# LoRA kernel, its tail: x and the product summed in PSUM for a tile and a half, and the last duo's split moved ahead

## The reference

```python
def _L0_cond_ref(x, A, B, adapter_ids):
    B_sel = B[adapter_ids]
    A_sel = A[adapter_ids]
    Bx = jnp.einsum('bni,bri->bnr', x, B_sel)
    out = jnp.einsum('bnr,bor->bno', Bx, A_sel)
    return out * SCALING          # SCALING = 1.0
x = x + _L0_cond_ref(x, L0_cond_A, L0_cond_B, itok_B_3_7)
```

## Time and profile before

| what | value |
|---|---|
| median of 3 runs | 93.06 us (93.05 to 93.09) |
| the profiled execution, whole time | 93.04 us |
| its span in the profile | 91.2 us |
| PE busy | 80.1 us (88%) |
| DVE busy | 59.7 us (65%) |
| ACT busy | 59.0 us (65%) |
| POOL busy | 60.3 us (66%) |
| DMA moved | 34.82 MB, mean 382 GB/s |

### The profile page before, as it was taken

One profiled execution on the slowest core, in us unless ns is written; L12 is line 12 of the kernel. 1 busy time (PEld: TensorE's weight loads), 2 busy tenths in 40 slices (PEclk: granted clock), 3 DMA queues, 4 the chain that ended last, 5 costly groups with the idle time before them and its releaser, 6 DMA issues.

```text
span 91.2 us, 3627 instructions
## 1 busy us (share of the span) xinstructions
PE 80.1 (88%) x1469; PEld 63.0 (69%) x1469; DVE 59.7 (65%) x106; ACT 59.0 (65%) x153; POOL 60.3 (66%) x136
## 2 busy tenths in 40 slices
PE   3999999999999999899999999999999999464400
PEld 3999988778687778587778687878787786322100
DVE  0039930359686768775959586776869696999900
ACT  1367698969696859396869596969695958131000
POOL 6000859999879697877878879797979793900000
PEclk9999999999999999999999999999999999999555
DMA  1899999999999999999999999999999999988890
GB/s 25 311 386 410 408 410 412 401 413 410 395 413 408 404 412 403 406 412 403 410 412 404 415 419 408 412 415 410 422 408 413 430 397 421 392 345 356 341 386 20
DMA packets 10193, 34.82 MB, mean 382 GB/s; under 512 B 834, under 2 KB 1858, under 8 KB 10178
## 3 DMA queue, kind: packets, MB, share of 16 engines
q1 hardware_dynamic: 10032, 34.08, 93.7%
q10 hardware_dynamic: 146, 0.52, 1.5%
HBM read 17.83 MB, written 16.78 MB: 380 GB/s over the span
## 4 chain that ended last, share of the span: by engine, by line
PE 85%; DVE 6%; issue 1%; ACT 1%; POOL 1%; POOLq 0%
PE t_bank L217 36%; PE y_banks L248 20%; PE bx_bank L228 20%; PE t_bank L187 5%; DVE x_all L361 4%; PE y_banks L206 4%; DVE bx_parts L352 2%; PE bx_bank L192 1%; ACT bx_parts L283 1%; POOL ident L140 0%; POOL ident L138 0%; POOLq L140 0%; POOLq L377 0%
## 5 line engine op out<-in xcount | busy, mean ns | idle before, releaser
L361 DVE TENSOR_TENSOR x_all<-y_banks,x_all 128x1024 f32<-128x1024 f32 x32 | 39.4, 1232 | 15.7 <-PE y_banks L248 15.1
L301 ACT COPY x_t<-t_bank 128x512 f32<-128x512 f32 x64 | 34.5, 592 | 13.9 <-PE t_bank L217 13.3
L166 POOL CAST a_duo<-a_table 128x512 fp32r x64 | 36.7, 615 | 3.1 <-PE y_banks L248 2.1
L217 PE MATMUL t_bank<-ident,x_all 128*128 128x128 f32 x256 | 34.9, 279 | 0.0
L156 POOL COPY b_duo<-b_table 128x256 f32 x64 | 22.8, 401 | 15.8 <-PE bx_bank L228 8.7
L217 PEld LDWEIGHTS t_bank<-ident,x_all 128*128 128x128 f32 x256 | 27.5, 141 | 7.0 <-issue 5.4
L248 PE MATMUL y_banks<-a_duo,bx_parts 64*128 64x512 f32 x128 | 20.6, 429 | 3.6 <-ACT bx_parts L283 3.2
L228 PE MATMUL bx_bank<-x_t,b_duo 128*32 128x64 f32 x1024 | 21.3, 222 | 0.0
L228 PEld LDWEIGHTS bx_bank<-x_t,b_duo 128*32 128x32 f32 x1024 | 16.1, 109 | 5.6 <-issue 5.2
L352 DVE TENSOR_TENSOR bx_parts<-bx_bank,bx_parts 32x64 fp32r<-32x64 f32 x64 | 14.1, 220 | 4.8 <-ACT bx_parts L316 3.7
L248 PEld LDWEIGHTS y_banks<-a_duo,bx_parts 64*128 64x128 f32 x128 | 10.9, 188 | 7.3 <-issue 3.8
(11 more groups left out here) (10 smaller groups left out, 4.9 us busy)
## 6 DMA issues: line engine op xcount, KB each, us to landing
out_y<-x_all SPq DMA_DIRECT2D x32, 512.0 KB, 13.2
x_all<-in_x SPq DMA_DIRECT2D x15, 1024.0 KB, 19.0
x_all<-in_x SPq DMA_DIRECT2D x2, 512.0 KB, 6.1
x_all<-in_B ACTq DMA_DIRECT2D x1, 512.0 KB, 4.3
x_all<-in_A SPq DMA_DIRECT2D x2, 256.0 KB, 4.8
id_row<-in_ids ACTq DMA_DIRECT2D x1, 0.2 KB
```

Of the source, the lines that this page charges most:

```text
L166: last = nc.gpsimd.tensor_copy(a_duo[duo % 2][:, k, :], a_table[:, bass.ds(adapters[k] * BANK, BANK)])
L217: last = nc.tensor.transpose(t_bank[unit % 2][:, c * P:(c + 1) * P], x_all[:, 2 * duo + tile, at:at + P], ident[:, :])
L301: nc.scalar.copy(x_t[duo % 2][:, half * HALF:(half + 1) * HALF, tile, :], t_bank[unit % 2][:, :].rearrange("p (c n) -> p c n", c=HALF)).th ...
L361: nc.vector.tensor_tensor(here, product, here, ALU.add).then_inc(y_drained, 1)
```

## The change

Only the tail is touched, duos 14 and 15. Line numbers of the changed kernel are higher by 9 on PE's loops, by 47 on ACT and by 56 on VectorE.

- Tile 29 (the second of duo 14) doesn't go through `y_banks` and VectorE any more. PE puts x itself into the two transpose banks, one matmul of the identity with 512 columns of x for each half (`x_into`), and adds the products of A onto it in the same banks. ACT copies the two sums to `x_all`, and the store waits for these copies (`sum_copied`).
- Tile 31 (the last) is cut in two. Its first half goes to `y_banks0` and VectorE as before, on 512 columns. Its second half is summed in `bx_bank0` as above and copied out by ACT.
- Tile 30 goes to `y_banks1` in place of `y_banks0`.
- ACT splits the last duo's B x (`split_high`) ahead of `double_parts` of duo 14, and VectorE does `split_rest` of duo 15 ahead of its add on tile 28.

The diff:

```diff
@@ -94,6 +94,8 @@
         parts_done = sem("parts_done")
         y_filled = sem("y_filled")
         y_drained = sem("y_drained")
+        sum_filled = sem("sum_filled")
+        sum_copied = sem("sum_copied")
 
         block = ctx.enter_context(nc.Block())
 
@@ -129,7 +131,14 @@
                     sp.wait_ge(a_filled, ADAPTERS)
                 sp.dma_start(x_all[:, first:end, :], rows[:, first:end, :]).then_inc(x_loaded[n], 16)
             for tile in range(TILES):
-                sp.wait_ge(y_drained, tile + 1)
+                if tile < TILES - 3:
+                    sp.wait_ge(y_drained, tile + 1)
+                elif tile == TILES - 3:
+                    sp.wait_ge(sum_copied, HALVES)
+                else:
+                    sp.wait_ge(y_drained, tile)
+                if tile == TILES - 1:
+                    sp.wait_ge(sum_copied, HALVES + 1)
                 sp.dma_start(out_rows[:, tile, :], x_all[:, tile, :]).then_inc(stored, 16)
             sp.wait_ge(stored, 16 * TILES)
 
@@ -269,9 +278,47 @@
                     transpose_unit(duo + 1, 2)
                     transpose_unit(duo + 1, 3)
                 down(duo, HALF, CHUNKS)
-                if duo:
+                if 0 < duo < DUOS - 1:
                     up(duo - 1)
-            up(DUOS - 1)
+            def product(bank, duo, k, h, start, stop):
+                ranks = slice(h * K_UP, (h + 1) * K_UP)
+                return nc.tensor.matmul(bank, bx_parts[duo % 2][ranks, k, :], a_duo[duo % 2][ranks, k, :],
+                                        start=start, stop=stop)
+
+            def x_into(bank, tile, h):
+                nc.tensor.matmul(bank, ident[:, :], x_all[:, tile, :].rearrange("n (o h) -> n h o", h=HALVES)[:, h],
+                                 start=True, stop=False)
+
+            before, end = DUOS - 2, DUOS - 1
+            for h in range(HALVES):
+                x_into(t_bank[h][:, :], TILES - 3, h)
+            pe.wait_ge(a_gathered, before + 1)
+            pe.wait_ge(parts_done, before + 1)
+            pe.wait_ge(y_drained, 2 * before - 1)
+            for s in range(PER_TILE):
+                for h in range(HALVES):
+                    last = product(y_banks[0][:, h * BANK:(h + 1) * BANK], before, s, h, s == 0, s == PER_TILE - 1)
+            last.then_inc(y_filled, 1)
+            for s in range(PER_TILE):
+                for h in range(HALVES):
+                    last = product(t_bank[h][:, :], before, PER_TILE + s, h, False, s == PER_TILE - 1)
+            last.then_inc(sum_filled, 1)
+
+            pe.wait_ge(a_gathered, end + 1)
+            pe.wait_ge(parts_done, end + 1)
+            pe.wait_ge(y_drained, 2 * before)
+            for s in range(PER_TILE):
+                for h in range(HALVES):
+                    last = product(y_banks[1][:, h * BANK:(h + 1) * BANK], end, s, h, s == 0, s == PER_TILE - 1)
+            last.then_inc(y_filled, 1)
+            pe.wait_ge(y_drained, 2 * before + 1)
+            for s in range(PER_TILE):
+                last = product(y_banks[0][:, 0:BANK], end, PER_TILE + s, 0, s == 0, s == PER_TILE - 1)
+            last.then_inc(y_filled, 1)
+            x_into(bx_bank[before % 2][:, :], TILES - 1, 1)
+            for s in range(PER_TILE):
+                last = product(bx_bank[before % 2][:, :], end, PER_TILE + s, 1, False, s == PER_TILE - 1)
+            last.then_inc(sum_filled, 1)
 
         @block.scalar
         def _(act):
@@ -325,13 +372,22 @@
                 if duo + 1 < DUOS:
                     copy_x(duo + 1, 0)
                     copy_x(duo + 1, 1)
+                if duo == DUOS - 1:
+                    split_high(duo)
                 if duo:
                     double_parts(duo - 1)
                 if duo + 1 < DUOS:
                     copy_x(duo + 1, 2)
                     copy_x(duo + 1, 3)
-                split_high(duo)
+                    split_high(duo)
             double_parts(DUOS - 1)
+            act.wait_ge(sum_filled, 1)
+            for h in range(HALVES):
+                nc.scalar.copy(x_all[:, TILES - 3, :].rearrange("n (o h) -> n h o", h=HALVES)[:, h],
+                               t_bank[h][:, :]).then_inc(sum_copied, 1)
+            act.wait_ge(sum_filled, 2)
+            nc.scalar.copy(x_all[:, TILES - 1, :].rearrange("n (o h) -> n h o", h=HALVES)[:, 1],
+                           bx_bank[(DUOS - 2) % 2][:, :]).then_inc(sum_copied, 1)
 
         @block.vector
         def _(dve):
@@ -361,12 +417,19 @@
                 nc.vector.tensor_tensor(here, product, here, ALU.add).then_inc(y_drained, 1)
 
             split_rest(0)
-            for duo in range(1, DUOS):
+            for duo in range(1, DUOS - 1):
                 add_x(duo - 1, 0)
                 split_rest(duo)
                 add_x(duo - 1, 1)
-            add_x(DUOS - 1, 0)
-            add_x(DUOS - 1, 1)
+            split_rest(DUOS - 1)
+            add_x(DUOS - 2, 0)
+            dve.wait_ge(y_filled, TILES - 2)
+            here = x_all[:, TILES - 2, :].rearrange("n (o h) -> n h o", h=HALVES)
+            product = y_banks[1][:, :].rearrange("n (h o) -> n h o", h=HALVES)
+            nc.vector.tensor_tensor(here, product, here, ALU.add).then_inc(y_drained, 1)
+            dve.wait_ge(y_filled, TILES - 1)
+            first_half = x_all[:, TILES - 1, :].rearrange("n (o h) -> n h o", h=HALVES)[:, 0]
+            nc.vector.tensor_tensor(first_half, y_banks[0][:, 0:BANK], first_half, ALU.add).then_inc(y_drained, 1)
 
 
 # ---- launch: one core; inputs and outputs as the reference has them ----
```

## The result

The changed kernel takes 93.28 us (median of 22 runs, 93.01 to 93.43) against 93.08 us for the kernel before in the same set (22 runs, 92.85 to 93.26). The ratio is 1.0018, 95% interval 1.0011 to 1.0026: by it 0.17 us slower. Two more sets, on other occasions, gave 1.0005 (0.9987 to 1.0022) and 1.0007 (0.9991 to 1.0022). So the last store's issue moved, and the time did not move down with it; whether it moved up by 0.1 to 0.2 us or not at all is at the edge of what can be measured; where the difference of the first set lies, the part on the cost of 0.17 us tells. The forecast was 93.05 and no change.

What follows compares the result with a forecast made beforehand. One DMA engine, behind by its own total, was taken to bound the kernel; tile 28's loss (0.93 us) cancels tile 29's gain for the others, so the sum is 0: 93.05 us, no change, range 92.6 to 93.3.

Steps and rivals of the forecast that it cites:

- What bounds the kernel: End of the span: one DMA engine of sixteen, behind by its own total, works alone over a microsecond, share 0.06.
- The slack that was read from the shares: Last stores: the last engine had tiles 29, 30 and 31 at hand each 1.6 us before it needed them.
- The sum of 0 for the change: Whole kernel: tile 28's loss cancels tile 29's gain and the last engine never waits; no change, chance 0.75.
- span 91.2, whole time 93.04: Last step of the sum: span and whole time with the change, against a median of 93.06, so 93.05 forecast.
- It never waits, and ends at 90.33: Last DMA engine in the changed tail: gets tiles 28 to 31 before needing them, so its end stays at 90.33.
- the landing of the last packet: End of the kernel: with small shifts between executions, the reason given for the forecast's own range, 92.9 to 93.2.
- The products with x: PE in the tail: identity times x on 512 columns, 0.85 us each; two take 1.7 us (1.0 to 2.3).
- The last store: Tile 31's store: issued at 85.4 us (85.0 to 85.9), 1.2 us earlier; SP's wait behind it 5.1 us.
- Tile 28 later by 0.93, the dry time only moved: Tile 28's add ends at 82.74, not 81.81; fifteen engines' dry time moves from 84.0-84.95 to 82.8-83.7.
- The end follows the last store: Rival, end of the kernel: the lone engine's lateness comes from the tail, so an earlier store gives 91.9; chance 0.13.
- x products that hold up tile 28: Rival, PE ahead of tile 28: slow x products (2.3 us each at the lower clock) delay its store, 94.3; chance 0.06.
- The instruction packets shift: Rival, DMA engines: last engine gains or loses 1.06 us of packet work, 94.1 or 91.9; chance 0.03 slower, 0.03 faster.

Runs made afterwards that it cites:

- the run with three spare adds: Kernel before with three spare VectorE adds of 128x1024, results unused, ahead of the last store's release (3.7 us planned delay): 95.33 us, ratio 1.0232.
- one add: Kernel before with one spare VectorE add of 128x1024, result unused, ahead of the last store's release: 93.11 us, ratio 1.0010.
- the three parts: Parts of the change, each alone in the kernel before: order of splits, ratio 0.9995; tile 29 by transpose banks and ScalarE, 0.9997; tile 31 cut in two, 1.0117.
- the part with the last tile alone: Kernel before with only tile 31 changed: second half summed with x in a down bank and copied by ScalarE: 94.35 us, ratio 1.0117.
- a version with fewer of them, at a lower precision: Kernel before with transposed x and gathered B kept in bf16, 7 instruction packets in place of 11: 91.40 us against 93.10, ratio 0.9820.
- the spare products: Kernel before with the change's three added fp32 products of 512 columns at its places on TensorE, results unused: 93.28 us, ratio 1.0030 without the run at 94.53.

## Why the prediction was right or wrong

*What bounds the kernel*: right. The lone engine is there in the stretches of all these kernels (0.06 or 0.07 at the end), and its end does not follow the stores: with last stores between 83.2 and 88.3 us the profiled executions, with tile 31 stored in one piece, have their last data at 90.3 to 90.6. The slack that was read from the shares, 1.6 us for tile 31, is what the run with three spare adds measured (4.4 us of delay in its profile, 2.8 paid; one add, none).

*The sum of 0 for the change*: right within 0.1 us for two of three sets and for two of the three parts, and short by 0.17 us for the first set, whose interval excludes zero. The step that failed is the last one of the sum: "span 91.2, whole time 93.04". It adds to the span the 1.84 us that lie outside it as if the change couldn't touch them, a term that I put at nothing without a reason. The runs show that it grew: 1.94 us on the mean in the first set against 1.83 in the other sets' runs of the kernel before, because half of all executions of the changed kernel have 1.95 to 2.05 us there, and none of 107 of the kernel before. Why three more products bring that stays open.

The step before it, "It never waits, and ends at 90.33", looks wrong in the profile after (90.57) and is not: 90.33 is one execution's end, the end differs by 0.3 us between executions of kernels with one and the same DMA work, and the mean spans agree within 0.03 us. That the one execution I read stood for the others was luck; I gave "the landing of the last packet" 0.15 us with nothing but it to go by.

*The products with x*: mis-sized. Forecast 0.85 each, with bounds of 0.51 and 1.16; measured 1.0 for the first two and 1.1 for the third. The row of `down` was the nearer of the two bounds, and I went to the middle. The trace is 0.15 to 0.25 above my value. It changed nothing, as the product was hidden by VectorE.

*The last store*: forecast 1.2 us earlier, measured 0.58 relative to tile 27's. The chain behind tile 28's add was short by 0.6: the pair in `y_banks0` 0.65 in place of 0.6, the product 1.1 in place of 0.85, the two last matmuls and the step to ACT 0.77 in place of 0.5. For the same reason SP waits 3.9 us behind it and not 5.1. It changed nothing either.

*Tile 28 later by 0.93, the dry time only moved*: right to 0.01 us for the store, and the dry stretch stands before tile 28's data as it was said. For a gain the store that ends the dry stretch, tile 28, would have to come earlier; the change makes that one later.

*The rivals.* "The end follows the last store" has fallen. "x products that hold up tile 28" did not occur. The lower clock that it reckoned with did, in a place I had not looked at: in the part with the last tile alone (0.50, 2.0 us for the product with x). "The instruction packets shift" did not occur either: there are 11 packets before and after. But it looked at the right thing. Without TensorE's program, and so without a packet, the loads and stores take 3.6 us less, and the time goes with the number of packets. The prediction had the row with eleven packets of 1.06 us and left them at a side remark.

## What to carry to other kernels

Before a tail is shortened, look at the DMA share of its last microseconds in short stretches: here a share of 0.06, one sixteenth, was a single DMA engine that was behind by its own total, and the slack of each store could be computed from its end backwards (1.6 us, as the run with three spare adds then measured). Where DMA engines are full throughout (1.02 to 1.03 here), count the instruction packets too: here a version with fewer of them, at a lower precision, was 1.7 us faster where a better tail brought nothing. When a difference of 0.2% is in question, split the time of every run into its span and the rest before the tail is blamed. And a piece of work that is put at the end of TensorE's program should be priced at the lower clock too: the product with x took 2.0 us at the end of the run with the last tile alone and of that with the spare products (0.50), and 1.1 in the whole change (1.00). What makes the clock fall these runs don't tell.

## What the runs showed of the hardware that I had not expected

With the DMAs alone and 0, 6 and 12 instruction packets of 16 KB (0.10 and 0.20 MB on the pages) the time was 89.50, 91.58 and 93.12 us, 0.30 us a packet; packets and matmuls were changed together. In the kernel before such a packet took 1.06 us of one DMA engine's time on the mean. By the small packets a transfer of 128 rows went to sixteen DMA engines (816 for 51 transfers) and one of 80 rows to sixteen as well (16 more); for one of 120 rows they fit fifteen (7 more), which the landed shares (9 more) leave unsure. The time outside the span, 1.83 us on the mean, was 1.95 to 2.05 in half of the changed kernel's executions. An fp32 product of 128x128 with 512 columns, read at every second number, took 1.0 to 1.1 us with the clock at 1.00 and 2.0 us at 0.50. DMA engines were not even without any program: with the DMAs alone three or four of them ended about one microsecond behind the others (share 0.82 at 86.0 to 86.2 us, 0.25 at 86.4 to 86.6, 0.15 at 87.0 to 87.2), for which no run here gives a reason.
